# Cross-attention over 12,544 keys: the second layer's first two key groups in one stage each

## The reference, cut to what matters

```
x = x + L0_xattn(layernorm(x), ctx, mask)     # softmax(q k^T + mask) v, q scaled by 1/4
x = x + L0_attn(layernorm(x), ...)            # linear attention, then a GELU MLP
x = x + L0_ffn(layernorm(x), ...)             # ternary gate, up, down
x = x + L1_xattn(layernorm(x), ctx, ctx) @ Wo + bo
x = x + L1_attn(layernorm(x), ...)            # RWKV
x = x + L1_ffn(layernorm(x), ...)             # ternary, conv, silu
```

## Time and profile before

| | us |
|---|---|
| median of 3 runs | 965.04 |
| lowest and highest | 963.46, 966.1 |
| profiled execution, its own time | 969.17 |
| its span in the trace | 966.3 |

### The profile page before, as it was taken

One profiled execution on the slowest core, in us unless ns is written; L12 is line 12 of the kernel. 1 busy time (PEld: TensorE's weight loads), 2 busy tenths in 40 slices (PEclk: granted clock), 3 DMA queues, 4 the chain that ended last, 5 costly groups with the idle time before them and its releaser, 6 DMA issues.

```text
span 966.3 us, 37466 instructions
## 1 busy us (share of the span) xinstructions
PE 924.5 (96%) x16290; PEld 572.3 (59%) x16291; DVE 755.6 (78%) x1610; ACT 697.8 (72%) x1005; POOL 398.6 (41%) x365
## 2 busy tenths in 40 slices
PE   7999999999999999999888899999999999999987
PEld 3455665665656566655563556666666666666666
DVE  5888888888888888967446988777777778777666
ACT  3678998998998899897563456666666666666752
POOL 4368888788888877886100010021202000110000
PEclk9999999999999999999997999999999999999999
DMA  8411201201211110123005001011101101000000
GB/s 337 165 42 67 88 26 68 90 24 68 89 60 55 67 58 8 68 91 134 6 26 193 2 2 46 3 45 46 45 4 46 46 3 46 14 3 3 3 1 6
DMA packets 14995, 53.08 MB, mean 55 GB/s; under 512 B 4336, under 2 KB 5744, under 8 KB 10992
## 3 DMA queue, kind: packets, MB, share of 16 engines
q1 hardware_dynamic: 14832, 50.70, 15.1%
HBM read 50.56 MB, written 0.13 MB: 52 GB/s over the span
## 4 chain that ended last, share of the span: by engine, by line
PE 83%; DVE 7%; issue 5%; ACT 3%; DMA 1%; POOL 0%; SPq 0%; DVEq 0%; POOLq 0%; ACTq 0%
PE ps_out L1599 18%; PE ps_scores L1578 16%; PE ps_proj L1501 15%; PE ps_proj L1516 14%; PE ps_max L1523 7%; PE ps_scores L1574 4%; DVE tile_max L1102 2%; ACT probs L821 1%; PE ps_proj L1523 1%; DVE probs L1194 1%; PE ps_scores L1516 1%; DMA bq<-in_L_xattn_bq 1%; DVE unread L1099 1%; PE ps_out L1477 1%; PE ps_max L1477 1%
## 5 line engine op out<-in xcount | busy, mean ns | idle before, releaser
L637 POOL TENSOR_TENSOR probs<-probs,masks 128x512 f32<-128x512 f32 x180 | 227.3, 1284 | 76.3 <-ACT probs L807 76.3
L815 ACT ACTIVATE probs<-probs 128x1024 f32<-128x1024 f32 x196 | 206.7, 1055 | 44.7 <-DVE probs L1183 34.1
L1578 PE MATMUL ps_scores<-q_pad,k_full 32*128 32x256 f32 x3072 | 237.3, 378 | 0.0
L1099 DVE CUSTOM_DVE_ANT_0 unread<-ps_max,masks 128x512 bf16<-128x512 f32 (+1 forms) x294 | 190.5, 675 | 49.1 <-PE ps_max L1523 48.2
L821 ACT ACTIVATE probs<-ps_scores 128x1024 f32<-128x1024 f32 x192 | 186.3, 1021 | 44.8 <-PE ps_scores L1578 44.4
L1599 PE MATMUL ps_out<-probs,values 128*32 128x128 f32 x6272 | 217.1, 277 | 1.6 <-DVE ps_out L1166 0.5
L1578 PEld LDWEIGHTS ps_scores<-q_pad,k_full 32*128 32x128 f32 x3072 | 187.0, 187 | 12.5
L1599 PEld LDWEIGHTS ps_out<-probs,values 128*32 128x32 f32 x6272 | 159.3, 110 | 57.3 <-issue 50.4
L1501 PE MATMUL ps_proj<-wv,ctx_t 128*32 128x256 f32 x2752 | 165.3, 381 | 0.2
L1523 PE MATMUL ps_max<-k_high,q_high 32*128 32x512 bf16 (+1 forms) x579 | 153.2, 382 | 8.5 <-DVE tile_max L1099 3.2
L1516 PE MATMUL ps_proj<-ctx_t,wk 128*32 128x512 f32 (+1 forms) x1360 | 159.8, 587 | 1.0 <-DVE tile_max L1099 0.8
(11 more groups left out here) (308 smaller groups left out, 940.8 us busy)
## 6 DMA issues: line engine op xcount, KB each, us to landing
ctx_t<-in_ctx_t SPq DMA_DIRECT2D x23, 1024.0 KB, 5.9
masks<-in_mask_n SPq DMA_DIRECT2D x12, 512.0 KB, 3.7
masks<-in_mask_t SPq DMA_DIRECT2D x12, 512.0 KB, 3.9
room_w<-in_L_attn_f_w SPq DMA_DIRECT2D x2, 1024.0 KB, 7.0
room_w<-in_L_ffn_w SPq DMA_DIRECT2D x2, 1024.0 KB, 8.1
ctx_t<-in_ctx_t SPq DMA_DIRECT2D x2, 512.0 KB, 5.7
room_w<-in_L_ffn_w_gate SPq DMA_DIRECT2D x1, 1024.0 KB, 11.1
room_w<-in_L_ffn_w_up SPq DMA_DIRECT2D x1, 1024.0 KB, 13.6
```

What stands on the lines that cost most here:

```text
L637: nc.gpsimd.tensor_tensor(p, p, three(mask_t[m % 2], GT)[:, t, :].unsqueeze(1).to_broadcast([P, 4, P]), ALU.add).then_inc(sig("bias_added" ...
L815: nc.scalar.activation(prob(T, half), prob(T, half), ACT.Exp).then_inc(sig(f"exp_done{half}"), 1)
L1099: ins = v.tensor_tensor_reduce(unread[:, j % 2, 0:width(m)], max_bank(m, j)[:, 0:width(m)], mask_n[m % 2][:, half_cols(m, half)], 1.0, -3e ...
L1578: last = mm(banks[g][:, D * c:D * (c + 1)], k_full[m % 3][rows, c, P * t:P * (t + 1)], q_pad[rows, c, :], start=False, stop=True, skip_gro ...
```

## The change

- `is_split` is false for every group, so a stage is a group and layer 1 has 13 stages. `CHAINS` is empty.
- All 32 maxima of group 13 are taken as 16 pairs before its first scores. In the loop, group 13's tiles have maxima of group 14 (and from tile 6 on of 15) alone.
- `BETWEEN` has nine units instead of thirteen, `BESIDE` seven instead of three, behind pairs 1, 3, 5, 7, 9, 11 and 13.
- Ahead of the first turn of maxima in layer 1 stand 7 idle products instead of 1, and 2 more behind it.
- Ramp: `FIRST_AT` has the units one place earlier, unit 1 comes behind the first four maxima, unit 11 behind the first tile's scores. The load of the query bias is issued right behind the query weights.
- In `maximum` on VectorE the waits for the mask and for the earlier maxima stand ahead of the wait for the product.

```diff
         def is_split(m):
-            return m in (NG, NG + 1)
+            return False
 
         def stage(m, t=0):
-            return m + max(0, min(m - NG, 2)) + int(is_split(m) and t >= SPLIT)
+            return m
...
-        CHAINS = {(NG, SPLIT - 2): NG + 1, (NG, 5): NG + 2, (NG, 7): NG + 3}
+        CHAINS = {}
...
             if m == NG:
-                own = ((2, 2, 2), (2, 2, 2), (2, 2, 0))[t] if t < SPLIT - 1 else own
-                now = ((0, 0, 0), (0, 0, 0), (0, 0, 4), (2, 2, 2), (2, 2, 2), (2, 2, 2), (2, 2, 2), (2, 2, 0))[t]
-            elif m == NG + 1:
-                now = (2, 2, 2) if t in (2, 4) else (2, 0, 2) if t < chain_at(m) else (2, 0, 0) if t == chain_at(m) else now
+                now = (2, 2, 2) if t in (1, 2, 3) else (2, 0, 2) if t < chain_at(m) else (2, 0, 0) if t == chain_at(m) else now
...
-            if m == NG:
-                ahead = (0, 0, 2) if t == size(m) - 1 else ahead
-            elif n + 2 < NG:
+            if n + 2 < NG:
                 ahead = (0, 0, 2) if t == chain_at(m) else (2, 0, 2) if t > chain_at(m) else ahead
...
-        FIRST_AT = ((2,), (3,), (4,), (5,), (6, 7), (8,), (9,), (10, 11))
+        FIRST_AT = ((1,), (2,), (3,), (4, 5), (6, 7), (8,), (9,), (10,))
-        BETWEEN = [("k", NG + 1, 0), ("k", NG + 1, 1), ("v", NG, 0), ("v", NG, 1), ("v", NG, 2), ("k", NG + 1, 2), ("k", NG + 1, 3),
-                   ("k", NG + 2, 0), ("v", NG, 3), ("v", NG + 1, 0), ("v", NG + 1, 1), ("v", NG + 1, 2), ("k", NG + 2, 1)]
-        BESIDE = [("k", NG + 2, 2), ("k", NG + 2, 3), ("v", NG + 1, 3)]
-        BESIDE_AT = (2, 5, 7)
+        BETWEEN = [("k", NG + 1, 0), ("k", NG + 1, 1), ("v", NG, 0), ("k", NG + 1, 2), ("k", NG + 1, 3), ("v", NG, 1),
+                   ("v", NG, 2), ("v", NG, 3), ("k", NG + 2, 0)]
+        BESIDE = [("k", NG + 2, 1), ("v", NG + 1, 0), ("k", NG + 2, 2), ("v", NG + 1, 1), ("k", NG + 2, 3), ("v", NG + 1, 2), ("v", NG + 1, 3)]
+        BESIDE_AT = (1, 3, 5, 7, 9, 11, 13)
...
             load_q_weights(0)
+            row(bq[0][:, :], "L0_xattn_bq", D, "q_bias0")
             load_k_weights(0)
             load_first_ctx(0)
-            row(bq[0][:, :], "L0_xattn_bq", D, "q_bias0")
...
                 if j == 0:
                     need("max_chain", stage(m))
+                    if m < NG:
+                        dve.wait_ge(sig(f"mask_n_loaded{m % 2}"), m // 2 * 16 + 16)
+                if m < NG:
+                    need("max_free", J - 1)
                 dve.wait_ge(sig("max_ready"), J + 1)
                 if m < NG:
-                    if j == 0:
-                        dve.wait_ge(sig(f"mask_n_loaded{m % 2}"), m // 2 * 16 + 16)
-                    need("max_free", J - 1)
...
                 else:
-                    for i in range(H // 2):
+                    for i in range(H):
                         pair_maximum(NG, i)
...
                 if l == 1:
-                    idle_products(1, ps_proj)
+                    idle_products(7, ps_proj)
                 turn_max(NG * l, ps_proj)
                 if l == 1:
-                    beside_read(2)
+                    for u in (len(BESIDE) - 2, len(BESIDE) - 1):
+                        if u % 2 == 0:
+                            beside_read(u)
+                    idle_products(2)
...
                         elif n > 0:
                             weigh(m - 1, size(m - 1) - 1)
+                        elif l == 0:
+                            first_in(len(FIRST) - 1)
```

## The result

The changed kernel took 971.74 us (median of 4, 971.61 to 972.97), the kernel before 965.57 beside it (4 runs, 963.46 to 967.57). The ratio is 1.0068 with an interval of 1.0051 to 1.0085: slower, by 6.2 us, where 959.7 was forecast. The profiled execution took 972.97, span 971.2; the span of before was 966.3.

A forecast was written before the change was run, and what follows sets the result against it. TensorE was taken to bound the kernel, with 83% of the chain of waits. The terms 0.9 + 0 - 3.9 + 9.6 - 11.9 sum to -5.3 us, from a median of 965.04 to 959.7, range 956.5 to 966.5.

The forecast's parts named there:

- Order of the mask and buffer waits: VectorE's layer 0 maxima: waits moved ahead of the product's are the same wait; 0 us, bounds 0 and -0.9.
- Ramp: Before layer 0's first scores: earlier start -1.3, place with two units +1.4, last key unit -0.3 and +1.1; sum +0.9 us.
- Between the layers: Small matrices between layers 0 and 1: 13 whole projections become 9, five savings; -3.9 us, bounds 0 and -6.9.
- The turn: Into layer 1: 16 pairs of maxima instead of 8 before the first scores, +9.1, slip 0.5; +9.6 us.
- The first two groups: Layer 1, groups 13 and 14: maxima, reductions, turns and decays leave the loop; 62.6 against 74.5 us, -11.9.
- Rival 1: Clock falls between the layers, output projection and key unit take twice as long: +2.7, 962.4 us; chance 0.20.
- Rival 2: Group 13 of layer 1 runs at half clock, all eight tiles cost 13.6: 973.3 us, slower; chance 0.15.
- Rival 3: Turn and ramp eat the gain: TensorE late in seven units (+2.3), ramp costs 2.5; 963.6 us; chance 0.12.

The follow-up runs named there:

- b_newwait: Kernel before with one edit: VectorE's layer 0 waits written mask, buffer, product instead of product, mask, buffer; 974.34 us, ratio 1.0093.
- a_oldwait: Changed kernel with the old order of waits (product first, then mask and buffer); 964.15 us, ratio 0.9996.
- a_passed: Changed kernel with one more, already passed wait (the buffer wait again) behind the wait for the product; no time given in the text.
- a_oldramp: Changed kernel with the ramp of before, new order of waits kept; 970.12 us, ratio 1.0063.
- a_both: Changed kernel with both the old ramp and the old order of waits; 961.52 us, ratio 0.9967.
- u11_back: Changed kernel with the old order of waits and the last key unit back ahead of the turn of the maxima; 962.76 us, ratio 0.9962.
- few_idle: a_both with 1 idle product ahead of the turn of layer 1's maxima instead of 7, none behind instead of 2; 964.31 us, ratio 0.9979.
- l1_first: bq_early with a long met wait written first ahead of every single maximum of layer 1; 967.26 us, ratio 1.0019.
- bq_early: a_both with the query bias loaded ahead of the key weights, none of the ramp's other edits; 960.30 us, ratio 0.9959.
- keep_warm: bq_early with an idle product in each of four gaps between the layers; 960.38 us, ratio 0.9958.
- ride: keep_warm with the wait that ends last written first at about a dozen places on VectorE or TensorE; 958.94 us, ratio 0.9947.

## Why the prediction was wrong, step by step

**Order of the mask and buffer waits (0, bounds 0 and -0.9): this is the step that failed.** Its reason was that "it is the same wait". It is another instruction that waits. Measured: 7.5 us from tile 0 to tile 97 in the kernel before alone (b_newwait), 7.6 by the medians in the changed kernel (a_oldwait), where 0 was forecast. Two parts of the reasoning were wrong. The bounds left out a loss, with no reason that excluded one. And "TensorE ends the chain and VectorE has slack" was read from shares. VectorE has slack on average, but one maximum in each tile starts when its product is done, and a product of TensorE behind the next scores waits for the bank that it frees. The chain of before has that wait too, with a piece of 0.09 us, and the prediction left it out.

**Ramp (+0.9).** The first maximum started at 12.13 in after, forecast 12.45. The place of two units and the order among the maxima cost 1.4 as estimated. The unit in tile 0 was the error: I charged TensorE's own time, 1.1, and it cost 2.15 between tiles 0 and 3 through GpSimd's queue, an engine that my step didn't name, less the 0.4 that it gave back ahead of the turn (26.48 to 26.04). With this unit and the new waits together, in after and a_passed, the clock fell in the ramp as well; in a_oldwait's and a_oldramp's profiles, with one of the two each, it did not. These are single profiles, so that the clock falls for this reason is not shown. In after's profile that is an estimated 3.1 us (12.62 to tile 97, less 7.4 for the waits and 2.15). In a_oldwait the five shortest of ten executions took 963.2 to 963.8 at 0.998 over the span, and the five others 964.5 to 966.7 at 0.996; where the clock fell in those five is not shown, and in the profile, one of the five shortest, it fell between the layers (0.86 in 472 to 484). By the medians a_oldwait is 2.6 over a_both; by their ratios to before, u11_back and a_both are level (0.9962 and 0.9967).

**Between the layers (-3.9).** From the first unit to the first pair are 43.7 us (475.05 to 518.78) against 47.8 in before (462.72 to 510.53), 4.1 less. Right as a sum; no run takes its five terms apart.

**The turn (+9.6).** Sixteen pairs took 18.19 us (518.78 to 536.97), the first scores start 1.95 later; +9.3 in all. Right, and so is the point on idle products: few_idle's profile loses 2.9 without them.

**The first two groups (-11.9).** 61.84 us against the 62.6 forecast, a gain of 12.65. Group 13 took 28.01 and group 14 33.83, forecast 28.7 and 33.9. Right as a difference of two profiles. But only 7.3 of it (69.10 to 61.84) is left where the clock holds on both sides; the rest is the clock, which fell in the profile of before. Here the way from the profile to the median was wrong. The profiled execution was 4.1 over the median, and I carried the whole difference over, though a large term of the sum was made of just that excess. With the clock held on both sides the layer 1 part is worth 7.3 less 5.3 (70.71 against 65.45 from tile 97 to layer 1's first scores), so 2.0, and its measured gain is 2.5 by the medians (a_both). Even with the two other parts at nothing the time would have been about 962.5 (an estimate, 2.5 under 965.04), and not 959.7.

**The rivals.** Rival 1 (the clock falls between the layers) is real in some executions: 0.72 in 472 to 484 in a_both and u11_back, 0.86 in a_oldwait and l1_first, but 1.00 in after, bq_early and few_idle. Its price in a_both was 2.2 us (72.94 against 70.69 from tile 97), forecast 2.7. Rival 2 gave the time nearest to the result, 973.3, by luck, for its mechanism did not happen: group 13 ran at 1.00 throughout. The Trainium skill's rule on cycling through PSUM banks ("TensorE: Matmul & The Clock Gate", section "A second HAM failure mode: psum-queue depth-cycling") would have it fall there; in this case's traces, after and a_both, it doesn't. Rival 3 (the turn and the ramp eat it) was half right, on the ramp.

What stays open: what makes up the 0.1 us. At the output projection the chain shows 0.02 for the semaphore instruction and 0.06 behind it, in front of the maximum with a mask it is 0.11 more than without; no run separates the parts. And that the clock held in all six executions of keep_warm is a fair sign, not a proof, that idle products hold it there.

## What to carry to other kernels

Where an instruction waits for two things, find out which wait the instruction itself carries (here the one written first), and give that place to the one that ends last. A met wait that went ahead of the instruction cost nothing here. Where it took the place of the wait that ended last, the instruction started 0.08 to 0.12 us later each time, which was 7 us over a layer. Look at such a wait even on an engine with slack, wherever another engine waits for the buffer that it frees. And before a profiled gain is carried to a median, see whether it is made of what the profiled execution lost by chance, above all a fall of the clock.

## What the runs showed of the hardware that was not expected

The start of the ramp differs from one execution to the next by over 3 us: tile 0 starts at 37.22 in bq_early's profile and at 40.57 in keep_warm's, whose ramps are the same. In keep_warm's the first context took 6.21 us to land, until 9.30. The same holds for before (38.29) and b_newwait (41.04). The rows are the first key unit: in after, and in b_newwait, where its context landed late.

```profile
8.08 1.92 PE L1509 MATMUL ps_scores<-ctx_t,wk 128*32 128x512 f32 x16
```

```profile
9.12 3.64 PE L1517 MATMUL ps_scores<-ctx_t,wk 128*32 128x512 f32 x16 [1.27 <-DMA ctx_t<-in_ctx_t]
```

The late start goes with a second loss: TensorE idles 1.27 us, and then the unit takes 3.64 us for the same 16 products. The view gives a granted clock of 1.00 for 8 to 12 us of both, but 1.00 is also what it gives where the trace has no record of the clock. The first record, of the full clock, begins at 7.86 in after and at 14.12 in b_newwait. In every trace here, single products of this unit that ended ahead of that first record took 1.03 to 1.06 us, and those well behind it 0.59 to 0.62: in u11_back, where it begins at 10.51, those that started at 8.2 to 9.1 took 1.06 and those from 10.63 on 0.59. Products of the same form took 1.06 as well in after at 56.2 to 57.9, where the clock is 0.50 (56 to 59). So the slow unit most likely ran at the lower of the two clock levels, with no record of it, and in keep_warm, where the record begins at 13.16, the whole unit took 3.64 us as well. A mean clock of 1.0 over the span does not tell of this stretch either. The 3 us are about what lies between the fastest and the slowest executions of keep_warm and ride; that the start makes that difference is not shown.
